# One shared latent unit per attention step, later loads, and the next step's first three scores ahead of the last products

## The reference

```python
xn = layer_norm(x, g1, b1)                      # context, 1601 rows of 128
ln_lat = layer_norm(latents, g2, b2)            # 64 rows
q = ln_lat @ Wq
kv = jnp.concatenate([xn, ln_lat], axis=1) @ Wkv
...
weight = jnp.einsum('bhld,bhnd->bhln', q * scale, k * scale)
weight = jnp.where(full_mask[:, None, None, :], weight, neg)
weight = jax.nn.softmax(weight.astype(jnp.float32), axis=-1)
out = jnp.einsum('bhln,bhnd->bhld', weight, v)
return out.transpose(0, 2, 1, 3).reshape(b, l, heads * dim_head) @ Wout
```

## Time and profile before

| | us |
|---|---|
| median of 3 runs | 2124.28 |
| lowest and highest | 2116.65, 2128.4 |
| profiled execution | 2114.37 |
| its span, first to last instruction | 2112.7 |
| mean granted clock of TensorE | 0.977 of full speed |

### The profile page before, as it was taken

The page is one execution under the profiler, slowest core; times in us unless marked ns, Lnnn a source line. Parts: engine busy times, 40 slices in busy tenths (PEclk is TensorE's granted clock), DMA queues, the critical chain, the costliest instruction groups (busy, mean ns, idle before and its releaser), DMA issues. The chain is left out here.

```text
span 2112.7 us, 38721 instructions
## 1 busy us (share of the span) xinstructions
PE 1972.5 (93%) x12154; PEld 1058.3 (50%) x12154; DVE 1716.3 (81%) x4135; ACT 1276.5 (60%) x2282; POOL 797.7 (38%) x761
## 2 busy tenths in 40 slices
PE   6899999999999999889798999999999999998886
PEld 6444544444444545533666545454545454544584
DVE  7889989898999887599666787879797978885657
ACT  4466666676757576444224786877777777776211
POOL 5465555555555560088001423333232323230000
PEclk9999999999999999999998999999999999999997
DMA  4232221222222110033104111111111111110100
GB/s 147 67 102 66 66 76 55 77 62 85 65 65 65 50 50 1 24 111 110 39 1 114 34 44 39 38 37 37 37 41 37 37 37 38 37 29 1 29 1 10
DMA packets 148172, 108.94 MB, mean 52 GB/s; under 512 B 120749, under 2 KB 136089, under 8 KB 148025
## 3 DMA queue, kind: packets, MB, share of 16 engines
q1 hardware_dynamic: 148024, 107.26, 17.9%
HBM read 65.15 MB, written 14.29 MB: 38 GB/s over the span
## 5 line engine op out<-in xcount | busy, mean ns | idle before, releaser
L1196 DVE TENSOR_TENSOR x_p_lo<-x_psum,x_p_hi 128x512 f16<-128x512 f32 (+2 forms) x896 | 604.6, 683 | 114.1 <-ACT x_psum L964 108.4
L963 ACT ACTIVATE x_p_hi<-x_psum 128x512 f16<-128x512 f32 (+2 forms) x480 | 286.9, 598 | 277.3 <-PE x_psum L805 274.9
L963 ACT ACTIVATE x_p_hi<-x_psum,x_bcol 128x512 f16<-128x512 f32 (+1 forms) x416 | 288.1, 693 | 155.2 <-PE x_psum L805 146.8
L824 PE MATMUL x_psum<-x_p_hi,x_x_both 128*128 128x512 f16 (+1 forms) x832 | 316.4, 380 | 17.8 <-DVE x_p_lo L1196 16.5
L803 PE MATMUL x_psum<-x_q,x_xT_both 128*128 128x512 f16 x832 | 316.4, 380 | 5.1 <-DMA x_q<-x_shift_rows 4.9
L805 PE MATMUL x_psum<-x_q,x_xT_both 128*128 128x512 f16 x832 | 315.3, 379 | 0.0
L804 PE MATMUL x_psum<-x_q,x_xT_both 128*128 128x512 f16 x832 | 315.3, 379 | 0.0
L826 PE MATMUL x_psum<-x_p_hi,x_x_both 128*128 128x512 f16 (+1 forms) x832 | 315.3, 379 | 0.0
L825 PE MATMUL x_psum<-x_p_lo,x_x_both 128*128 128x512 f16 (+1 forms) x832 | 315.3, 379 | 0.0
L1135 DVE CUSTOM_DVE_ANT_0 x_junk<-x_psum,x_brow 128x512 bf16<-128x512 f32 (+2 forms) x512 | 279.8, 586 | 11.1 <-PE x_psum L882 9.5
L964 ACT ACTIVATE x_psum<-x_psum 128x512 f32<-128x512 f32 (+2 forms) x480 | 285.1, 594 | 0.6
(11 more groups left out here) (459 smaller groups left out, 3556.7 us busy)
## 6 DMA issues: line engine op xcount, KB each, us to landing
x_x_both<-context_rows SPq DMA_DIRECT2D x32, 832.0 KB, 5.4
context_rows<-x_x SPq DMA_DIRECT2D x16, 832.0 KB, 3.5
x_raw<-in_ctx SPq DMA_DIRECT2D x16, 768.0 KB
ssm_c_row<-ssm_bc_rows SPq DMA_DIRECT2D x16, 512.0 KB, 4.2
ssm_b_wide<-ssm_bc_rows SPq DMA_DIRECT2D x7, 512.0 KB, 3.5
x_mrow<-in_mask_BxS_bk SPq DMA_DIRECT2D x16, 200.1 KB
x_Wkv<-in_L_xattn_Wkv SPq DMA_DIRECT2D x4, 512.0 KB, 5.2
x_xT_both<-context_rows SPq DMA_TRANSPOSE x96, 3.9
```

What stands on the lines that cost most here:

```text
L824: pe.matmul(out, v_hi, p_hi[r][rows, :], start=start, stop=False)
L963: act.activation(p_hi[r][rows, :], score[r][rows, :], ACT.Exp, scale=SCORE_UNIT, **bias).then_inc(p_hi_ready, 1)
L1196: v.tensor_tensor(p_lo[r][rows, :], score[r][rows, :], p_hi[r][rows, :], ALU.subtract).then_inc(p_lo_ready, 1)
```

## The change

- **One shared unit for the latents.** `STEPS` becomes 27. Unit 26 holds both halves of the columns: half 0 in partitions 0 to 63 of the bank, half 1 in 64 to 127. `scores` makes six matmuls of 64 output rows, alternating between the halves; the exponentials and `p_lo` work on 128 partitions once. `products` makes six matmuls of 64 rows, alternating, into the two banks of `aux`. For this each half needs the latents' values on its own partitions, so `lat_hi` and `lat_lo` get a second copy with the halves crossed, written by four DMAs in the prologue, and `latp` holds both.
- **Ring.** 27 isn't a multiple of 4, so `user_before` says which unit used a bank last: the first three units of a step follow units 24, 25 and 26.
- **Scores ahead.** `HOLD` is 2: scores 0, 1 and 2 of the next step all stand ahead of the last products.
- **Turning.** `TURN_BY` is LAST - 4, which is 22 as before, while the step ends a unit earlier; the items keep their units (`turn` at 19 and 22).
- **Late loads.** The rest of the turned context and the rows of step b + 1 are loaded within step b (after six scores, and after the front part) instead of at the end of step b - 1.

```diff
-STEPS = 2 * (KT + 1)
+STEPS = 2 * KT + 1
...
+    def user_before(u):
+        return u - RING if u >= RING else LAST - (LAST - u) % RING - STEPS
...
-    HOLD = 1
-    TURN_BY = LAST - AHEAD - HOLD - 1
+    HOLD = 2
+    TURN_BY = LAST - 4
...
+                for x in (held["lat_hi"], held["lat_lo"]):
+                    for k in range(2):
+                        here, there = (slice(L * q, L * q + L) for q in (k, 1 - k))
+                        sp.dma_start(x[there, 1, :, :], x[here, 0, :, :]).then_inc(held["lat_crossed"], 16)
...
+                rest = at.has_next and not (at.first and at.par == 0)
+                if rest:
+                    wait_alone(sp, s_ready, at.half + 2 * AHEAD)
+                    load_xT_rest(sp, at.n, at.npar)
                 if at.has_next:
                     rows_out(at)
...
                     load_xT_front(sp, at.b + 2, at.par)
+                if rest:
+                    wait_alone(sp, pv_done, at.half)
+                    load_x(sp, at.n, at.npar)
                 if at.has_next:
                     rows_in(at)
-                if at.has_next2:
-                    wait_alone(sp, s_ready, at.half + 2 * KT)
-                    sp.wait_ge(held["prep_done"], 1)
-                    load_xT_rest(sp, at.b + 2, at.par)
-                    wait_alone(sp, pv_done, at.half + 2 * KT)
-                    sp.wait_ge(held["prep_done"], 1)
-                    load_x(sp, at.b + 2, at.par)
...
+                if j == KT:
+                    if par == 0:
+                        pe.wait_ge(pair_ready, i + 1)
+                    rows = slice(L * par, L * par + L)
+                    halves = [(score[u % RING][L * k:L * k + L, :].rearrange("p (c k) -> p c k", k=P),
+                               slice(k * NC_ // 2, (k + 1) * NC_ // 2)) for k in range(2)]
+                    for out, chunks in halves:
+                        pe.matmul(out, latTp[0][:, rows], q_hi[1][par][:, chunks, :], start=True, stop=False)
...
+                    sides = [(aux[:, k * HALF:(k + 1) * HALF], slice(L * k, L * k + L)) for k in range(2)]
+                    hi, lo = ([x[rows, (at.par + k) % 2, :] for k, (_, rows) in enumerate(sides)] for x in latp)
+                    for (out, rows), v_hi in zip(sides, hi):
+                        pe.matmul(out, v_hi, p_hi[r][rows, :], start=True, stop=False)
...
-                    if u == LAST - 1:
+                    if u == LAST:
                         pe.wait_ge(aux_free, at.free(("lat", 0)) - 2)
...
-                    act.wait_ge(pv_done, at.half + u - RING + 1)
+                    act.wait_ge(pv_done, at.half + user_before(u) + 1)
```

More of the change, by code:

```diff
@@ new lines, in scores @@
+                if j == KT:
[6 more added lines that the diff above has]
+                        pe.matmul(out, latTp[0][:, rows], q_hi[1][par][:, chunks, :], start=True, stop=False)
+                    for out, chunks in halves:
+                        pe.matmul(out, latTp[0][:, rows], q_lo[1][par][:, chunks, :], start=False, stop=False)
+                    for out, chunks in halves:
+                        ins = pe.matmul(out, latTp[1][:, rows], q_hi[1][par][:, chunks, :], start=False, stop=True)
+                    ins.then_inc(s_ready, 1)
+                    return
@@ L802, in scores @@
+                chunks = slice((u % 2) * NC_ // 2, (u % 2 + 1) * NC_ // 2)
+                k_hi, k_lo = xT_hi[par][:, j * P:(j + 1) * P], xT_lo[par][:, j * P:(j + 1) * P]
                 out = score[u % RING].rearrange("p (c k) -> p c k", k=P)
-                pe.matmul(out, k_hi, q_hi[s][par][:, chunks, :], start=True, stop=False)
-                pe.matmul(out, k_hi, q_lo[s][par][:, chunks, :], start=False, stop=False)
-                pe.matmul(out, k_lo, q_hi[s][par][:, chunks, :], start=False, stop=True).then_inc(s_ready, 1)
+                pe.matmul(out, k_hi, q_hi[0][par][:, chunks, :], start=True, stop=False)
@@ L807, in products @@
+                pe.matmul(out, k_hi, q_lo[0][par][:, chunks, :], start=False, stop=False)
+                pe.matmul(out, k_lo, q_hi[0][par][:, chunks, :], start=False, stop=True).then_inc(s_ready, 1)
             def products(u, at):
@@ L811, in products @@
                 if j == KT:
-                    rows = slice(L * at.par, L * at.par + L)
-                    out, v_hi, v_lo, start, stop = aux[:, (u % 2) * HALF:(u % 2) * HALF + HALF], latp[0][rows, :], latp[1][rows, :], True, True
-                else:
-                    rows = slice(0, P if j < CT else TAIL)
-                    out, v_hi, v_lo = acc[u % 2], x_hi[at.par][rows, j, :], x_lo[at.par][rows, j, :]
-                    start, stop = j == 0, j == CT
+                    sides = [(aux[:, k * HALF:(k + 1) * HALF], slice(L * k, L * k + L)) for k in range(2)]
+                    hi, lo = ([x[rows, (at.par + k) % 2, :] for k, (_, rows) in enumerate(sides)] for x in latp)
+                    for (out, rows), v_hi in zip(sides, hi):
+                        pe.matmul(out, v_hi, p_hi[r][rows, :], start=True, stop=False)
+                    for (out, rows), v_hi in zip(sides, hi):
+                        pe.matmul(out, v_hi, p_lo[r][rows, :], start=False, stop=False)
+                    for (out, rows), v_lo in zip(sides, lo):
+                        ins = pe.matmul(out, v_lo, p_hi[r][rows, :], start=False, stop=True)
+                    ins.then_inc(pv_done, 1)
+                    return
+                rows = slice(0, P if j < CT else TAIL)
+                out, v_hi, v_lo = acc[u % 2], x_hi[at.par][rows, j, :], x_lo[at.par][rows, j, :]
+                start, stop = j == 0, j == CT
                 if u == 0:
@@ L1079, in body @@
                     if masked:
-                        mask_col(at.n, at.npar, at.ni, None if at.first and at.par == 0 else at.half - 2)
+                        mask_col(at.n, at.npar, at.ni, None if at.first and at.par == 0 else at.half - (STEPS - 2 * KT))
                     if at.par == 0:
```

36 lines of the change are left out of this document (16 added, 20 removed).

## The result

| | before | changed |
|---|---|---|
| median of 4 runs, us | 2125.3 | 2098.76 |
| lowest and highest | 2116.65, 2128.4 | 2093.13, 2099.67 |
| profiled execution | 2114.37 | 2099.67 |

The ratio is 0.9883, 95% interval 0.9862 to 0.9903: faster by 1.2%. The predicted time was 2101.0 and the range 2085 to 2117. The number came out; not every step behind it did, and that needs the traces.

The account below looks back on a forecast made before the run. TensorE (93% busy) and VectorE (81%) bound the kernel, with the bound changing hands. Savings 5.7 + 0.9 + 7.0 + 3.2 + 4.9 + 1.7 = 23.4 took the 2112.7 span to 2089.3, scaled to 2100.8; range 2085 to 2117.

Parts of the forecast that it names:

- Score unit free, S(26) in the hole: Step ends: dropping score unit 27 saves 0; unit 26's six score matmuls (1.30 if serial) fit TensorE's wait of 1.45 to 1.51.
- Rival B: Step ends: holes close by themselves, so all six unit-27 matmuls per step come off, 42 us; time 2083; chance 8%.
- Rival C: Unit 26's scores: weight loads of 64-column matmuls not hidden, 0.5 later at each of 30 hand-overs; time 2118; chance 6%.
- P(26) at 0.65 with 0.18 around it: Unit 26's products: six 64-row matmuls run in pairs, taking 0.65 plus 0.18 of gaps, with 1.30 as other bound.
- rivals A and D: A: unit 26's products run serially, 1.30, time 2112, 15%. D: narrow units don't pipeline, 2.9 each, time 2215, 4%.
- Rival E: Hand-overs: third score ahead waits longer or shift chain lengthens, giving back the gain; 0 to 8 us, 2118 to 2124; 11%.
- x1's even ends and the odd ends outside the loop, 0.87 each: Hand-overs of dense TensorE: 8 x 0.87 = 7.0 at x1's even ends; outside-loop odd ends 4.9 (0.78 each in x0).
- Late loads at 0: Loads of turned rows, now issued within the step: priced at 0, with at least 3 us of reserve.
- The last steps, 2 x 0.87 = 1.7: Last step of each stage: loses one product unit and its gaps, 0.87 each, 1.7 in all.
- Back edges, 8 x 0.4 = 3.2: Odd ends at the loop's back edge, four per stage: the next step's first subtraction comes 0.40 earlier, 3.2 in all.
- p_lo(0) starts at T + 0.13 + 2.87: Back edge: VectorE's first subtraction starts 3.00 after the step's first score matmul instead of 3.40, 2.87 behind the copy.
- x0's even ends, 7 x 0.81 = 5.7: Even step ends in x0: VectorE's first subtraction and all behind it move 0.81 earlier; 5.7 in all.

Follow-up runs that it names:

- p26_twice: Changed kernel with the six product matmuls of unit 26 issued twice; 2106.37 us.
- hold1: Changed kernel with HOLD set back from 2 to 1; 2121.06 us.
- flat_after: Changed kernel with pairs 1 to 5 of each stage written out, so no hardware loop is left; 2086.29 us, ratio to the kernel before 0.9831.
- copy_late: Changed kernel with VectorE's copy of an odd step's sums moved behind the next step's first p_lo subtraction; 2091.03 us.
- stats_later: Changed kernel with VectorE's context statistics in odd steps of x0 moved one unit later; 2087.74 us, ratio to the kernel before 0.9828.
- p26_row: Changed kernel with the six product matmuls of unit 26 issued row half by row half instead of alternating; 2100.87 us.
- s26_row: Changed kernel with the six score matmuls of unit 26 issued column half by column half instead of alternating; 2101.44 us.
- s26_twice: Changed kernel with the six score matmuls of unit 26 issued twice; 2102.2 us.
- flat_stats: Changed kernel with the pairs written out and x0's odd-step statistics one unit later; 2075.98 us, ratio to the kernel before 0.9792.

## Why the prediction was right, and where it wasn't

- **Score unit free, S(26) in the hole:** right, but for x1's first even end, which has no hole. S(26) to P(24) is 2.06 and 2.01 (said: 2.1 to 2.2), and a doubled S(26) changed nothing in the two attentions. Rival B fell with it: the hole didn't close by itself, for the projection still hangs on the output matmuls. Rival C as well: the 64-column weight loads are not exposed.
- **P(26) at 0.65 with 0.18 around it:** right, 0.75 to S(3), no matter in which order; rivals A and D fell. Rival E too: P(26) stands at T + 2.04 as computed, so S(2) ahead of it doesn't wait, and the shift's chain is as long as it was. `p26_twice` put a unit's price at 0.65 and confirmed where it is paid.
- **x1's even ends and the odd ends outside the loop, 0.87 each:** right, 0.85.
- **The turning:** right; turning to S(0) 3.58 to 3.62. **Late loads at 0:** right in sum, and no maximum waits for a transfer. **Crossing transfers at 0:** no price shows. GpSimd waits 3.7 for one of them, but step 0 of x0 begins at 72.8 in the changed kernel, 70.7 to 73.2 in its variants, and 71.6 and 71.1 in the two profiles of before.
- **The last steps, 2 x 0.87 = 1.7:** too small; 1.16 came off each (4.45 to 3.29), 2.3 in all. TensorE is dense there, so the score unit pays too.
- **Back edges, 8 x 0.4 = 3.2:** wrong. The step that failed is "p_lo(0) starts at T + 0.13 + 2.87": I took the pause behind the copy for a constant and shifted it. The copy did come earlier (T + 0.21), but the pause grew to 3.20 and 3.71, and the term is a loss of 0.5. `hold1`, `flat_after` and `copy_late` show that the pause is the loop's and begins with the end of VectorE's last work before the jump. It isn't a constant: 2.18 in the earlier trace rows, 2.42 to 2.64 in x0 and 2.88 to 3.04 in x1 of the changed kernel, 2.28 to 2.51 at all eight back edges of `hold1`. The late loads have a part in x1 (0.4 in the row shown). Why else it is longest there is open; `hold1` has the late loads too. The profile had shown the pause, and the 0.88 outside; I counted it as given, where it was the next limit. I had also set the test, "I am wrong if S(0) to P(0) stays above 4": it does, at 9 of 30 hand-overs, the eight back edges and, by the clock, the first even end of x0 (5.10).
- **x0's even ends, 7 x 0.81 = 5.7:** mis-sized. p_lo(0) came even earlier than said (T + 2.07 for 2.25), but "all behind it moves by 0.81" left the statistics at their length beside GpSimd's adds. p_lo(0) to p_lo(1) grew from 2.57 to 3.03 and 0.53 is left. `stats_later` shows that this work, where it stands, costs 1.6 at each of these ends. How much of that is GpSimd's part no run separates; the growth itself is argued from the lengths of the statistics in the traces.
- **The first even end of x0** lost 0.8 in place of gaining 0.81, from TensorE's clock (below).

Added up over the two attentions: the terms without the last steps say 21.7, the traces 14.1. Of the 7.6, 3.7 are the back edges and 3.3 x0's even ends, with the clock's share in it. With the last steps (2.3) and step 0 of x1 (0.4) the traces have 16.8 where the sum had 23.4.

The forecast of 2101 still came out at 2098.8, since more than the mechanism lies between the medians: they are 22 to 26 apart, 5 to 10 more than the traces have. That much is luck of the forecast. The code outside the attentions differs in length from one execution to the next: middle and tail are 532.5 and 542.0 in the two profiles of before. But it isn't luck of these four runs alone. The median span less the two attentions of the profile is 657 to 662 for the kernel before, and 647 to 654, mostly 651, for the changed kernel and its eleven variants. Of the 6 or more between them, 2.7 are the last steps and step 0 of x1. The others have no cause that a trace shows: the parts without attention steps take 552 to 563 in those twelve profiles, and 554 and 563 in the two of before. So the mechanism gives about 17 us, 0.8%, and the rest is not explained by it. The range was right to be wider than the sum's own error.

## What to carry to other kernels

When a saving lets a step start earlier, look at what the next engine does between there and the first thing waited for, and price that as a limit of its own. A loop's back edge is such a limit: an engine that waits for another right ahead of its jump, as VectorE did here, pays the jump afterwards in full; move the waiting instruction behind the first work of the next body, or write the loop out. And keep small VectorE operations with two SBUF inputs away from a critical spot where GpSimd is adding.

## What the runs showed of the hardware

- **The jump on VectorE.** Between the last work of a body and the first of the next lie 2.1 to 3.4 us (80 back edges in the ten kernels with the copy ahead of the jump), where the same hand-over of the changed kernel written out waits 1.07 in x0, for ScalarE only. The Trainium skill, "Advanced Engine Details and Errata", section on control flow timing, gives about 51 ns for a branch and 108 for one with a comparison; the shortest pause is about twenty times the longer of the two, so the branch alone doesn't make it, and for a loop's price the measurement decides. A mechanism for it is not shown here.
- **VectorE beside GpSimd.** The same five operations over 13 columns take 0.17 to 0.18 each where GpSimd is idle, but up to 1.22 while it adds; p_lo, which reads one input from PSUM, is 0.67 to 0.69 in both. The Trainium skill, "SBUF — State Buffer", section on the two sides of SBUF, says that a VectorE operation with two SBUF inputs and a GpSimd operation that reads SBUF exclude each other for a whole instruction. The trace agrees: the statistic of 1.22 lies beside the add of 1.26, and one of 0.68 beside the next, of 0.73.
- **Two half-array chains run together in either order** (0.75 for six matmuls, where three of 64 rows took 0.75 before). The Trainium skill, "TensorE: Matmul & The Clock Gate", section on packing small matmuls, says that matmuls start and end strictly in program order; by that the half-by-half order would have been longer, and `p26_row` is not. Its records have the first matmul of the second half 0.01 after the first of the first half, ahead of two that come earlier in the program; the measurement decides.
- **The clock after the first step.** In the changed kernel TensorE idled 1.60 ahead of S(0) of step 1 in x0 (1.42 before). From 119.4 to 122.8 the granted clock is 0.51, the lower level, 1.2 GHz, and starts are 0.43 apart in place of 0.22. The query item comes 1.64 later than in the kernels whose clock stayed up there (T + 7.04 for 5.40).

```profile
118.74 0.39 PE L825 MATMUL x_psum<-x_q,x_xT_both 128*128 128x512 f16 x1 [1.60 <-DMA x_q<-x_shift_rows]
...
120.58 0.63 PE L825 MATMUL x_psum<-x_q,x_xT_both 128*128 128x512 f16 x1
121.01 0.63 PE L826 MATMUL x_psum<-x_q,x_xT_both 128*128 128x512 f16 x1
```

  The fall came in some kernels after such a pause and not in others (1.51 with it in `p26_row`, 1.54 without in `s26_row`, 1.66 without in `copy_late`), so the length of the pause alone doesn't decide. It stayed up in `s26_row`, `s26_twice`, `copy_late`, `stats_later` and `flat_stats`; that is the 1.6 named above.
